# Sorting a token-choice expert layer in three stages instead of two

## The chip, the cores and the metric

The kernel runs on one core of one Trainium2 chip. The metric is device microseconds for one execution. One execution of each kernel is also taken by the hardware profiler, and its trace gives the rows below.

## The reference

One decoder layer over `x` of 2048 tokens by 256 features, with a context of 1601 rows:

```python
x = layernorm(x + linear_attention(x))            # 8 heads of 64
x = layernorm(x + cross_attention(x, ctx))        # 16 heads of 16
probs = softmax(x @ gate_w.T)                     # 16 experts
top_w, top_idx = top_k(probs, 4); top_w /= sum(top_w)
expert_e(x) = (silu(x @ w1[e].T) * (x @ w3[e].T)) @ w2[e].T    # hidden size 128
x = layernorm(x + sum_j top_w[j] * expert_top_idx[j](x) + shared_expert(x))
```

The change is in the last two lines, and in how they are woven into the cross attention ahead of them.

## The kernel before

The work has three parts in time: the linear attention (up to about 250 us), the cross attention (to about 802 us), and the experts (to the end).

**Cross attention.** Queries come in 4 chunks of 512 tokens, heads in 4 groups G of each chunk, keys in 13 tiles: 4 x 4 x 13 = 208 steps, 52 for each chunk (the text calls a step of the last chunk "step 9", and so on). In a step, `scores` makes four score tiles in a ring of banks, ScalarE takes their exponential (L937), and `weigh` (L1163) multiplies them with the values two steps later. Beside this TensorE makes two units of scores for a later group, and VectorE reduces them to a maximum (`read_max`, L1466). These units are 17 steps ahead, so that in the last chunk VectorE has them only up to step 34, and in the last group (from step 39) `weigh_whole` (L1177) takes wider tiles. When a group is through, `copy_num` on ScalarE (L852) empties the sum bank behind two of the four exponentials of the group's second step, and `weigh` of the next group waits for it. SyncE then moves the sums (`move_num`) and their denominators (`move_den`); VectorE inverts the denominators (`invert`, L1527).

**Gate and sort.** Behind each chunk stand the projection, the layer norm and the gate for its 512 tokens. Each token chooses 4 experts. A token's row is copied 4 times into DRAM (`sorted_d`), sorted by expert, in tiles of 128 rows that each belong to one expert. Tokens of the first three chunks are one batch (63 tiles, 12 token tiles), the last chunk another (31 tiles, 4 token tiles). For a batch `ranks` counts on TensorE how many choices of an expert stand ahead, `first_slots` and `slot_ends` work out on VectorE where each expert begins, `slot_of_choice` and `all_slots` give each choice its row, and `tile_owners` says which expert a tile has. The owners go to DRAM and back as one row of SBUF (`write_owner`, `load_owner`), since TensorE's sequencer reads them from one partition. GpSimd then issues one indirect DMA for each token tile and choice (`scatter`, L677); ahead of each round of choices it marks the rows (`mark`), which waits until the round before has landed. For the first batch these are 48 scatters, from step 32 of the last chunk on.

**Experts.** `WORK` is a fixed list of 110 tiles: 10 of the shared expert, the 63 of the first batch, 6 shared, the 31 of the second batch. Its index is i. All engines go through it in order. SyncE loads the sorted rows 6 tiles ahead (`load_tile`), and the first tile of a batch waits for all its scatters; from the thirteenth expert tile on, a load also waits until the result of an earlier tile has landed. GpSimd scatters each result back to its tokens (`give`, L685) at i + 3. The last chunk's projection, norm, gate and sort are placed at fixed i (6 to 35, and `SCATTER_AT` 37 to 67 on GpSimd). From i = 77 (`COMBINE_AT`) a token tile's four results are loaded (`load_given`), added, normalised and stored. The queue of SyncE is one list in program order, as are those of the other engines:

```python
if s == CHUNK_STEPS * (CHUNKS - 1) + 36: write_owner(0)
...
move_num(CHUNKS * GROUPS - 1)
move_den(CHUNKS * GROUPS - 1)
for i in range(-X_AHEAD, len(WORK) + BEHIND):
    if 0 <= i + X_AHEAD < len(WORK): load_tile(i + X_AHEAD)
```

On VectorE the last group's `invert` stands at i = 0, between the activations of tiles 1 and 2, and the last division at i = 4. On GpSimd `inverse_deviation` of chunk 2 (L665) stands ahead of the first scatter.

## Time and profile before

| | |
|---|---|
| median of 3 runs | 1096.03 us (1095.07 to 1097.78) |
| the profiled execution | 1086.56 us |
| its span | 1084.7 us |
| mean granted TensorE clock | 0.940 |
| TensorE busy | 951.4 us (88%) |
| VectorE busy | 732.9 us (68%) |
| ScalarE busy | 648.0 us (60%) |
| GpSimd busy | 254.6 us (23%) |

The span is the time from the first to the last instruction of the profiled execution; its own time stands 1.9 us above. The busy shares are means over three parts with different limits, so the views by stretch of time say more than this table.

### The profile page before, as it was taken

The page shows a single profiled execution, that of the slowest core. Times are in us where ns is not written, and L with a number is a line of the kernel's source. Part 1 is how long each engine was busy: PE and PEld are TensorE (multiplying, and loading weights), DVE is VectorE, ACT ScalarE, POOL GpSimd, SP SyncE. Part 2 cuts the span into 40 slices and gives each one's busy share as a digit, 9 for nine tenths or more (in the row PEclk, how much of TensorE's full clock was granted, in tenths as well). Part 3 has the DMA queues.
Part 4 walks back from the last instruction along what each step waited for, and adds up shares of the span by engine and source line. Part 5 has one row for each costly group of instructions (what it writes and reads, how often), then busy time and mean ns, then how long its engine had stood idle before and what let it go on. Part 6 is the DMA issues. An engine that isn't in the chain of part 4 may idle for free.

```text
span 1084.7 us, 19088 instructions
## 1 busy us (share of the span) xinstructions
PE 951.4 (88%) x6868; PEld 521.9 (48%) x6868; DVE 732.9 (68%) x1171; ACT 648.0 (60%) x1403; POOL 254.6 (23%) x306
## 2 busy tenths in 40 slices
PE   6997998779999999999999999998990698988890
PEld 2454566334444444444444444443340586776670
DVE  0206886798999998989989899889120343324773
ACT  1322223118888887878878788777870265654560
POOL 1006113600000000200002000000465255773654
PEclk9999999859999999999999999999895799999996
DMA  9007892200322112112211010011642246554763
GB/s 346 8 1 179 101 129 92 94 5 2 100 81 86 42 50 84 37 35 58 86 55 27 8 27 22 25 53 50 142 148 75 86 142 137 158 157 148 242 214 131
DMA packets 75800, 99.29 MB, mean 92 GB/s; under 512 B 17566, under 2 KB 58784, under 8 KB 75390
## 3 DMA queue, kind: packets, MB, share of 16 engines
q1 hardware_dynamic: 64252, 73.73, 26.8%
q0 software_dynamic: 7584, 20.79, 5.4%
q10 hardware_dynamic: 3872, 3.56, 1.0%
q8 instruction: 57, 0.93, 0.4%
q14 instruction: 35, 0.29, 0.1%
HBM read 52.45 MB, written 43.35 MB: 88 GB/s over the span
## 4 chain that ended last, share of the span: by engine, by line
PE 60%; DVE 17%; DMA 8%; issue 7%; POOL 6%; ACT 2%; SPq 0%; POOLq 0%; DVEq 0%; ACTq 0%
PE psum L1163 16%; PE psum L1053 13%; DVE mpart L1466 9%; PE psum L1149 7%; PE psum L1318 6%; POOL sorted_d L677 4%; PE psum L982 3%; PE psum L1336 3%; PE psum L1015 3%; DMA x_in<-sorted_d 2%; DMA given_d<-y_out,x_in 2%; PE psum L1279 2%; DMA sorted_d<-x_rows,slots 2%; PE psum L1103 1%; PE psum L1187 1%
## 5 line engine op out<-in xcount | busy, mean ns | idle before, releaser
L937 ACT ACTIVATE region<-psum 128x512 f32<-128x512 f32 (+1 forms) x832 | 448.6, 610 | 132.0 <-PE psum L1149 117.6
L1466 DVE TENSOR_REDUCE mpart<-psum 128x2 f32<-128x1024 f32 x384 | 461.7, 1222 | 39.4 <-PE psum L1053 36.4
L1163 PE MATMUL psum<-region 128*32 128x256 f32 (+1 forms) x3120 | 251.8, 395 | 7.4 <-ACT numT L852 7.4
L1053 PE MATMUL psum<-kstack,qstack 63*128 63x512 f32 (+1 forms) x1024 | 223.0, 463 | 19.9 <-DVE mpart L1466 19.5
L1053 PEld LDWEIGHTS psum<-kstack,qstack 63*128 63x128 f32 x1024 | 92.9, 194 | 194.0 <-issue 123.7
L1149 PE MATMUL psum<-qstack,kstack 64*128 64x512 f32 (+1 forms) x832 | 176.1, 412 | 0.1
L1683 DVE SCALAR_TENSOR_TENSOR silu_h<-tanh_h,psum 128x128 f32<-128x128 f32 x110 | 31.6, 287 | 150.7 <-ACT tanh_h L907 149.4
L1149 PEld LDWEIGHTS psum<-qstack,kstack 64*128 64x128 f32 (+1 forms) x832 | 111.3, 184 | 17.6 <-ACT region L937 14.5
L1163 PEld LDWEIGHTS psum<-region 128*32 128x32 f32 (+1 forms) x3120 | 62.2, 108 | 118.1 <-issue 75.7
L1318 PE MATMUL psum<-w_all,xT_in 128*128 x376 | 103.3, 399 | 3.8 <-issue 1.7
L685 POOL DMA_INDIRECT given_d<-y_out,x_in x94 | 93.4, 994 | 44.8 <-ACT y_out L921 27.3
L718 POOL TENSOR_TENSOR attnT<-num_c,den_c 128x512 f32<-128x512 f32 x7 | 8.9, 1278 | 357.7 <-DMA den_c<-den_d 357.6
L1279 PE MATMUL psum<-ident,x_in 128*128 128x128 f32 x188 | 38.0, 285 | 48.9 <-DMA x_in<-sorted_d 48.8
L901 ACT ACTIVATE xT_in<-psum 128x256 f32<-128x256 f32 x110 | 41.4, 378 | 59.9 <-PE psum L1279 59.7
L1318 PEld LDWEIGHTS psum<-w_all,xT_in 128*128 128x128 f32 x376 | 67.1, 198 | 12.4 <-issue 6.3
L677 POOL DMA_INDIRECT sorted_d<-x_rows,slots x64 | 62.3, 974 | 32.8 <-issue 29.6
L907 ACT ACTIVATE tanh_h<-psum 128x128 f32<-128x128 f32 x110 | 30.5, 277 | 54.2 <-PE psum L1318 53.8
L1336 PE MATMUL psum<-w_all,actT 128*128 x188 | 58.2, 393 | 0.3 <-ACT actT L913 0.3
L1279 PEld LDWEIGHTS psum<-ident,x_in 128*128 128x128 f32 x188 | 26.7, 148 | 61.8 <-issue 53.8
L921 ACT ACTIVATE y_out<-psum,x_in 128x256 f32<-128x256 f32 x94 | 44.5, 473 | 12.2 <-PE psum L1336 3.4
L665 POOL TENSOR_TENSOR rstd<-var_eps,half_neg 128x1 f32<-128x1 f32 (+1 forms) x20 | 14.4, 721 | 143.9 <-DVE var_eps L1559 73.5
L817 ACT ACTIVATE region<-region 128x512 f32<-128x512 f32 x16 | 10.1, 630 | 54.6 <-DVE region L1493 54.6
(172 smaller groups left out, 937.5 us busy)
## 6 DMA issues: line engine op xcount, KB each, us to landing
x_in<-sorted_d SPq DMA_DIRECT2D x94, 129.0 KB, 2.5
sorted_d<-x_in SPq DMA_DIRECT2D x7, 1548.0 KB, 7.3
given<-given_d SPq DMA_DIRECT2D x16, 512.0 KB, 4.6
qstack<-qparts_d SPq DMA_DIRECT2D x96, 64.0 KB, 2.3
kstack<-kparts_d SPq DMA_DIRECT2D x6, 800.5 KB
qparts_d<-region SPq DMA_DIRECT2D x4, 1024.0 KB, 4.1
kparts_d<-region SPq DMA_DIRECT2D x4, 800.5 KB, 10.1
xT<-in_xT SPq DMA_DIRECT2D x1, 2048.0 KB, 9.2
```

The costliest lines, as they stand in the source:

```text
L677: pool.indirect_dma_start(out=sorted_d[int(t >= GATE_FIRST)][:, :], out_offset=bass.IndirectOffsetOnAxis(ap=slots[:, t, j:j + 1], axis=0), ...
L685: pool.indirect_dma_start(out=given_d[int(v >= FIRST_SLOT[1])][:, :], out_offset=bass.IndirectOffsetOnAxis(ap=x_in[:, v % X_SLOTS, DIM:DIM ...
L901: act.activation(xT_in[:, i % 3, :], turn_bank("tile", i)[:, 0:DIM], ACT.Copy).then_inc(xT_copied, 1)
L921: act.activation(y_out[:, v % Y_SLOTS, :], bank(2 + i % 2)[:, 0:DIM], ACT.Copy, scale=x_in[:, v % X_SLOTS, DIM + 1:DIM + 2]).then_inc(y_co ...
L937: act.activation(prob[0:rows_of, s % 3, j, :], ring(n)[0:rows_of], ACT.Exp).then_inc(ring_read, 1)
L1053: mm = pe.matmul(bank(unit_bank(u) + side)[:, at * w:(at + 1) * w], qstack[rows_of, buffer(G), p, t * P:(t + 1) * P], kstack[rows_of, g * ...
L1149: pe.matmul(ring(n)[0:r], kstack[rows, g * PAIRS + p, kt * P:kt * P + r], qstack[rows, buffer(G), p, :], start=True, stop=True).then_inc(r ...
L1163: mm = pe.matmul(bank(NUM_BANK)[VW * j:VW * (j + 1), q], vals[0:r, g, kt, j, :], prob[0:r, s % 3, j, q], start=(kt == 0 and half == 0), st ...
L1279: mm = pe.transpose(turn_bank("tile", i)[:, k * P:(k + 1) * P], rows[:, k * P:(k + 1) * P], ident[:, :])
L1318: mm = pe.matmul(bank(6 + i % 2)[:, 0:2 * HID], xT_in[:, i % 3, k * P:(k + 1) * P], part_of(kind, v, k), start=(k == 0), stop=(k == DK - 1))
L1336: pe.matmul(bank(2 + i % 2)[:, 0:DIM], actT[:, i % 2, :], part_of(kind, v, DK), start=True, stop=True).then_inc(y_done, 1)
L1466: dve.tensor_reduce(mpart[:, G % 2, qt, :, p, n], both, X, ALU.max).then_inc(max_read, 1)
```

## The change

1. There are three sorting stages. Stage 0 holds the tokens of chunks 0 and 1 (8 token tiles), stage 1 those of chunk 2, stage 2 those of chunk 3. Stages 0 and 1 fill the same 63 tiles: an expert's choices of stage 1 first fill the room left in its tiles of stage 0, and the rest goes into more tiles behind (`open_more`). The order of these tiles is therefore not by expert alone, and `tile_owners` counts twice for this batch.
2. In the last chunk VectorE works out stage 0 at steps 7, 8 and 9, stage 1 at step 34, the owners at step 42; the ranks are made at steps 4 and 32. GpSimd issues 32 scatters for stage 0 in halves of 4 token tiles, then 16 for stage 1 in halves of 2, and each half has its own semaphore, so that `mark` waits for the same half of the round before. The deviation of chunk 2 is placed behind the third half.
3. The owners are worked out on all partitions along the free axis, straight into the row that TensorE's sequencer reads; the two DMAs through DRAM go.
4. `WORK` is reordered: 4 shared, 32 expert tiles, 6 times (1 shared, 3 expert), 13 expert, 6 times (1 shared, 2 expert), 19 expert. The loads of its first 14 entries (10 expert tiles) stand at step 50 of the last chunk in SyncE's queue, ahead of the last group's `move_num` and `move_den`. The scatters of stage 2 are at i = 37 to 59, 2 in 3 tiles, with 8 marks.
5. `copy_num` stands behind one exponential instead of two.
6. One semaphore for four experts' weights instead of one for each.

```diff
+STAGES = 3
+STAGE_OF = (0, 0, 1, 2)
+STAGE_BATCH = (0, 0, 1)
+STAGE_TILES = tuple(TPC * STAGE_OF.count(s) for s in range(STAGES))
+STAGE_FIRST = tuple(TPC * STAGE_OF.index(s) for s in range(STAGES))
+STAGE_HALF = tuple(n // 2 for n in STAGE_TILES)
...
-FIRST_SHARED = 10
-WORK = ([("shared", t) for t in range(FIRST_SHARED)] + [("expert", v) for v in range(SLOT_TILES[0])]
-        + [("shared", t) for t in range(FIRST_SHARED, TILES)]
-        + [("expert", v) for v in range(SLOT_TILES[0], ALL_SLOTS)])
+def mixed(pattern, shared, expert):
+    return [("shared", next(shared)) if kind == "s" else ("expert", next(expert)) for kind in pattern]
+_shared, _expert = iter(range(TILES)), iter(range(ALL_SLOTS))
+WORK = mixed("s" * 4 + "e" * 32 + "seee" * 6 + "e" * 13 + "see" * 6 + "e" * 19, _shared, _expert)
...
+LOADED_EARLY = 14
...
-                        + [(20, "x2T", 0), (21, "x2T", 1), (23, "logits", 0), (24, "logits", 1), (30, "rank", 0)])
+                        + [(4, "rank", 0), (20, "x2T", 0), (21, "x2T", 1), (23, "logits", 0), (24, "logits", 1),
+                           (32, "rank", 1)])
...
-        COMBINE_AT = {77 + (8 * t) // 3: t for t in range(GATE_FIRST)}
-        SCATTER_AT = {37 + 2 * k: divmod(k, TPC) for k in range(TOPK * TPC)}
+        COMBINE_AT = {78 + (8 * t) // 3: t for t in range(GATE_FIRST)}
+        SCATTER_AT = {37 + (3 * k) // 2: divmod(k, TPC) for k in range(TOPK * TPC)}
...
-            def write_owner(b):
-                sp.wait_ge(owner_ready, b + 1)
-                sp.dma_start(owner_d[b:b + 1, :].rearrange("o p -> p o"), owner[:, b:b + 1]).then_inc(owner_written, 16)
-            def load_owner(b):
-                sp.wait_ge(owner_written, 16 * (b + 1))
-                sp.dma_start(owner_row[0:1, b, :], owner_d[b:b + 1, :]).then_inc(owner_loaded, 16)
...
-                        sp.wait_ge(scattered, 16 * TOPK * (FIRST_TOKEN[b] + TOKEN_TILES[b]))
+                        for stage in range(STAGES):
+                            if STAGE_BATCH[stage] == b:
+                                for half in range(2):
+                                    sp.wait_ge(scattered[stage][half], 16 * TOPK * STAGE_HALF[stage])
...
-                if s == CHUNK_STEPS * (CHUNKS - 1) + 36:
-                    write_owner(0)
-                if s == CHUNK_STEPS * (CHUNKS - 1) + 45:
-                    load_owner(0)
+                if s == STEPS - 2:
+                    for i in range(LOADED_EARLY):
+                        load_tile(i)
...
-                if 0 <= i + X_AHEAD < len(WORK):
+                if LOADED_EARLY <= i + X_AHEAD < len(WORK):
                     load_tile(i + X_AHEAD)
-                if i == 36:
-                    write_owner(1)
-                if i == 42:
-                    load_owner(1)
...
+            def mark(stage, half, j):
+                n = STAGE_HALF[stage]
+                at = STAGE_FIRST[stage] + half * n
+                first = at - FIRST_TOKEN[STAGE_BATCH[stage]]
+                if j >= 1:
+                    pool.wait_ge(scattered[stage][half], 16 * j * n)
                 link(pool.iota(x_rows[:, at:at + n, DIM:DIM + 1].bitcast(I32).rearrange("p t o -> p (t o)"),
-                               pattern=[[P * TOPK, n]], base=j, channel_multiplier=TOPK))
+                               pattern=[[P * TOPK, n]], base=first * P * TOPK + j, channel_multiplier=TOPK))
...
+            def sort_half(stage, half, j):
+                mark(stage, half, j)
+                for t in range(STAGE_HALF[stage]):
+                    scatter(stage, half, STAGE_FIRST[stage] + half * STAGE_HALF[stage] + t, j)
+            def sortable(stage):
+                pool.wait_ge(x2_ready, STAGE_FIRST[stage] + STAGE_TILES[stage])
+                pool.wait_ge(slots_ready, stage + 1)
...
-            pool.wait_ge(x2_ready, GATE_FIRST)
-            pool.wait_ge(slots_ready, 1)
+            sortable(0)
             for j in range(TOPK):
-                if j >= 1:
-                    pool.wait_ge(scattered, 16 * j * GATE_FIRST)
-                mark(0, j)
-                for t in range(GATE_FIRST):
-                    scatter(t, j)
-                if j == 1:
-                    divide(CHUNKS - 1, 0)
+                for half in range(2):
+                    sort_half(0, half, j)
+                    if j == 1 and half == 0:
+                        inverse_deviation(c_var, c_rstd, CHUNKS - 2, TPC)
+            sortable(1)
+            for j in range(TOPK):
+                for half in range(2):
+                    sort_half(1, half, j)
+            divide(CHUNKS - 1, 0)
...
+                    half, first = divmod(t, STAGE_HALF[2])
+                    if j == 0 and t == 0:
+                        sortable(2)
+                    if first == 0:
+                        mark(2, half, j)
+                    scatter(2, half, GATE_FIRST + t, j)
...
-                    if j == 2:
+                    if j == 1:
...
-                pe.wait_ge(owner_loaded, 16 * (b + 1))
+                pe.wait_ge(owner_ready, b + 1)
...
-                    if v < EXPERTS:
-                        pe.wait_ge(ld_we[v], 16 * 3)
+                    if v < EXPERTS and v % 4 == 0:
+                        pe.wait_ge(ld_we[v // 4], 16 * 3 * 4)
...
+            def open_tiles(stage):
+                rank_known(stage)
+                n = STAGE_TILES[stage]
+                link(dve.tensor_scalar(tiles_of[:, :], rank[:, n, :], (P - 1) / 2, 1.0 / P, ALU.add, ALU.mult))
+                link(dve.tensor_scalar(tiles_of[:, :], tiles_of[:, :], ROUND, ROUND, ALU.add, ALU.subtract))
+                link(dve.tensor_scalar(tiles_of[:, :], tiles_of[:, :], 1.0, None, ALU.max))
+                link(dve.tensor_tensor_scan(ends[:, :], tiles_of[:, :], zero_gate[:, 0, :], 0.0, ALU.add, ALU.add))
+                link(dve.tensor_tensor(start[:, :], ends[:, :], tiles_of[:, :], ALU.subtract))
+                link(dve.tensor_scalar(start[:, :], start[:, :], float(P), None, ALU.mult))
+                if stage == 0:
+                    link(dve.tensor_copy(count[:, :], rank[:, n, :]))
+                    link(dve.tensor_scalar(room[:, :], tiles_of[:, :], float(P), None, ALU.mult))
...
+            def open_more(stage):
+                rank_known(stage)
+                n = STAGE_TILES[stage]
+                link(dve.tensor_tensor(tiles_of[:, :], rank[:, n, :], count[:, :], ALU.add))
+                link(dve.tensor_tensor(tiles_of[:, :], tiles_of[:, :], room[:, :], ALU.subtract))
+                link(dve.tensor_scalar(tiles_of[:, :], tiles_of[:, :], 0.0, (P - 1) / 2, ALU.max, ALU.add))
+                link(dve.tensor_scalar(tiles_of[:, :], tiles_of[:, :], 1.0 / P, None, ALU.mult))
+                link(dve.tensor_scalar(tiles_of[:, :], tiles_of[:, :], ROUND, ROUND, ALU.add, ALU.subtract))
+                link(dve.tensor_tensor_scan(more_ends[:, :], tiles_of[:, :], zero_gate[:, 0, :], 0.0, ALU.add, ALU.add))
+                link(dve.tensor_scalar(more_ends[:, :], more_ends[:, :], ends[:, EXPERTS - 1:EXPERTS], None, ALU.add))
+                link(dve.tensor_tensor(jump[:, :], more_ends[:, :], tiles_of[:, :], ALU.subtract))
+                link(dve.tensor_scalar(jump[:, :], jump[:, :], float(P), None, ALU.mult))
+                link(dve.tensor_tensor(jump[:, :], jump[:, :], room[:, :], ALU.subtract))
+                link(dve.tensor_tensor(jump[:, :], jump[:, :], start[:, :], ALU.subtract))
...
+            def slot_of_choice(stage):
+                n = STAGE_TILES[stage]
+                r, hot, past = rank[:, 0:n, :], one_hot[:, 0:n, :, :], over[:, 0:n, :]
+                if stage == 1:
+                    link(dve.tensor_tensor(r, r, by_token(count[:, :], n), ALU.add))
+                    link(dve.tensor_tensor(past, r, by_token(room[:, :], n), ALU.is_ge))
+                    link(dve.tensor_tensor(past, past, by_token(jump[:, :], n), ALU.mult))
+                    link(dve.tensor_tensor(r, r, past, ALU.add))
+                link(dve.tensor_tensor(r, r, by_token(start[:, :], n), ALU.add))
...
+            def passed(b, to, after):
+                n = SLOT_TILES[b]
+                link(dve.tensor_tensor(
+                    over[:, 0:n, :], by_token(after, n),
+                    tile_no[:, 0:n].rearrange("p (t o) -> p t o", o=1).broadcast_to([P, n, EXPERTS]), ALU.is_le))
+                link(dve.tensor_reduce(to, over[:, 0:n, :], X, ALU.add))
+            def tile_owners(b):
+                n = SLOT_TILES[b]
+                first, other = who[:, 0, 0:n], who[:, 1, 0:n]
+                passed(b, first, ends[:, :])
+                if b == 0:
+                    link(dve.tensor_scalar(other, first, EXPERTS - 0.5, -float(EXPERTS), ALU.is_ge, ALU.mult))
+                    link(dve.tensor_tensor(first, first, other, ALU.add))
+                    passed(b, other, more_ends[:, :])
+                    link(dve.tensor_tensor(first, first, other, ALU.add))
+                link(dve.tensor_scalar(first, first, float(EXPERTS - 1), float(W_PARTS), ALU.min, ALU.mult))
+                link(dve.tensor_scalar(other, first, W_PARTS * BELOW - 0.5, float(W_PARTS * W_GAP), ALU.is_ge, ALU.mult))
+                dve.tensor_tensor(owner_row[:, b, 0:n], first, other, ALU.add).then_inc(owner_ready, 1)
             def activate(i):
                 h = bank(6 + i % 2)
...
-                    if at == 31:
-                        first_slots(0)
-                        slot_ends(0)
-                    if at == 32:
+                    if at == 7:
+                        open_tiles(0)
+                    if at == 8:
                         slot_of_choice(0)
+                    if at == 9:
                         all_slots(0)
-                    if at == 33:
+                    if at == 34:
+                        open_more(1)
+                        slot_of_choice(1)
+                        all_slots(1)
+                    if at == 42:
                         tile_owners(0)
             for i in range(-AHEAD, len(WORK) + BEHIND):
                 if i == 27:
                     gate_chosen(CHUNKS - 1)
                 if i == 31:
-                    first_slots(1)
...
                 if i == 31:
-                    first_slots(1)
+                    open_tiles(2)
                 if i == 32:
-                    slot_ends(1)
+                    slot_of_choice(2)
                 if i == 33:
+                    all_slots(2)
+                if i == 35:
                     tile_owners(1)
-                if i == 34:
-                    slot_of_choice(1)
-                if i == 35:
-                    all_slots(1)
                 if i - 2 in COMBINE_AT:
                     give_out(COMBINE_AT[i - 2])
                 if i in COMBINE_AT:
```

## Rows read from the trace of the kernel before

**Rows 1.** The page's clock in 40 slices, and the waits from 780 us on.

```profile
PEclk9999999859999999999999999999895799999996
PE psum L1279 <- DMA x_in<-sorted_d: 48.8, 7, 34.1
```

**Rows 2.** Timeline of TensorE: start, duration, instructions, idle before and its releaser.

```profile
850.00 0.66 PE L1279 MATMUL psum<-ident,x_in 128*128 128x128 f32 x2 [34.14 <-DMA x_in<-sorted_d]
...
915.96 0.41 PE L1279 MATMUL psum<-ident,x_in 128*128 128x128 f32 x2 [4.37 <-DMA x_in<-sorted_d]
```

**Rows 3.** Timeline of GpSimd, out of the first batch's 48 scatters.

```profile
759.87 1.23 POOL L677 DMA_INDIRECT sorted_d<-x_rows,slots  x1 [0.45 <-POOL x_rows L674]
...
770.87 0.97 POOL L677 DMA_INDIRECT sorted_d<-x_rows,slots  x1 [2.17 <-issue]
...
785.36 0.15 POOL L672 IOTA x_rows<- 128x12 int32 x1 [8.47 <-DMA sorted_d<-x_rows,slots]
...
845.37 0.97 POOL L677 DMA_INDIRECT sorted_d<-x_rows,slots  x1 [0.31 <-issue]
```

**Rows 4.** Timeline of SyncE's queue.

```profile
802.88 0.60 SPq L482 DMA_DIRECT2D den<-numT  x1
...
847.81 6.58 SPq L546 DMA_DIRECT2D x_in<-sorted_d  x12
```

**Rows 5.** The view by tile of numT: durations in ns, and who waited for it.

```profile
L852 ACT ACTIVATE numT<-psum x16: 597/605/605, 278.3 to 802.3; 128x512 f32<-128x512 f32 x16
...
  PE psum L1163: 7.4, 13
```

**Rows 6.** Timeline of VectorE around the first batch's sort, and the last inversion.

```profile
752.29 0.35 DVE L1639 TENSOR_TENSOR over<-rank,steps_of 128x192 f32<-128x192 f32 x1
...
758.66 0.19 DVE L1676 CAST slots<-which 128x48 int32<-128x48 f32 x1
...
761.88 0.16 DVE L1659 TENSOR_TENSOR owner<-small 128x1 int32<-128x1 f32 x1
...
764.73 0.21 DVE L1523 STREAM_TRANSPOSE negT<-negmax 128x32 f32<-128x32 f32 x1
...
806.44 0.24 DVE L1527 RECIPROCAL den<-den 128x16 f32<-128x16 f32 x1
```

**Rows 7.** Timeline of VectorE in steps 9 to 12, at step 17 and at step 19.

```profile
681.50 9.88 DVE L1466 TENSOR_REDUCE mpart<-psum 128x2 f32<-128x1024 f32 x8
...
710.43 0.17 DVE L1559 TENSOR_SCALAR var_eps<-meanvar 128x4 f32<-128x4 f32 x1
...
715.19 1.30 DVE L1555 TENSOR_SCALAR x_rows<-x_rows,meanvar,rstd 128x256 f32<-128x256 f32 x4
```

**Rows 8.** The view by tile of rank, its multiply by one_hot (ns).

```profile
L1669 DVE TENSOR_TENSOR one_hot<-one_hot,rank x2: 425/692/959, 756.7 to 905.7; 128x768 f32<-128x768 f32 x1, 128x256 f32<-128x256 f32 x1
```

**Rows 9.** The view by tile of owner_d, and busy time by window.

```profile
DMA to landing us min/median/max: 8.3/8.6/9.0
912.00:914.00 2.00, 0.00 (x0) 0.00 (x0) 0.00 (x1) 0.10 (x1) 1.69 (x2) 1.00 0.86 45
```

**Rows 10.** The chain that ended last: a result on its way to DRAM.

```profile
986.64 3.39 DMA given_d<-y_out,x_in
```

**Rows 11.** Windows (PE, PEld, DVE, ACT, POOL busy, clock, DMA share, GB/s).

```profile
757.00:763.00 6.00, 3.70 (x32) 1.88 (x30) 5.46 (x11) 2.28 (x5) 2.87 (x5) 0.75 0.37 107
850.00:875.00 25.00, 24.77 (x122) 20.45 (x123) 11.98 (x40) 12.16 (x41) 5.95 (x6) 0.89 0.30 85
```

**Rows 12.** Timeline of ScalarE: the tanh of tiles 43, 55, 78 and 79, of 110.

```profile
923.93 0.28 ACT L907 ACTIVATE tanh_h<-psum 128x128 f32<-128x128 f32 x1 [0.34 <-PE psum L1318]
...
943.46 0.28 ACT L907 ACTIVATE tanh_h<-psum 128x128 f32<-128x128 f32 x1 [0.34 <-PE psum L1318]
...
990.24 0.28 ACT L907 ACTIVATE tanh_h<-psum 128x128 f32<-128x128 f32 x1 [0.48 <-PE psum L1318]
997.60 0.28 ACT L907 ACTIVATE tanh_h<-psum 128x128 f32<-128x128 f32 x1 [2.76 <-PE psum L1318]
```

More of the change, by code:

```diff
@@ L240, in decoder_layer @@
         y_out = sb("y_out", [P, Y_SLOTS, DIM])
-        one_hot = sb("one_hot", [P, GATE_FIRST, TOPK, EXPERTS])
-        rank = sb("rank", [P, GATE_FIRST + 1, EXPERTS])
-        over = sb("over", [P, EXPERTS, GATE_FIRST])
-        ends = sb("ends", [P, 2, EXPERTS])
+        one_hot = sb("one_hot", [P, STAGE_TILES[0], TOPK, EXPERTS])
+        rank = sb("rank", [P, STAGE_TILES[0] + 1, EXPERTS])
+        over = sb("over", [P, SLOT_TILES[0], EXPERTS])
+        who = sb("who", [P, 2, SLOT_TILES[0]])
+        tiles_of, ends, start, room, count, more_ends, jump = (
+            sb(name, [P, EXPERTS]) for name in ("tiles_of", "ends", "start", "room", "count", "more_ends", "jump"))
         def sems(*names):
```

133 lines of the change are left out of this document (48 added, 85 removed).

## The prediction

> **What bounds the kernel now.** I read the clock in slices first. In slices 30 and 31 (about 813 to 868 us) it falls to 0.5 and 0.7 [rows 1]: TensorE has nothing to do there. The waits name it: TensorE waited 48.8 us in 7 places for sorted rows, once for 34.1 us [rows 1]. The timeline puts that wait at 816 to 850 us [rows 2], behind the shared tiles that can run without sorted rows. The queue of GpSimd shows why: the scatters start at 759.9 us and the last is issued at 845.4 us, 48 of them [rows 3], and SyncE's loads start 1.5 us behind it [rows 4]. So the sort of three chunks is too late by 34 us, and what ends it is GpSimd's issue, one scatter each 1.27 us.
>
> Elsewhere the bound is different. In the cross attention VectorE runs without a pause (8 reductions in 9.88 us, [rows 7]), so whatever is put on it before step 34 lengthens the step. In the experts the pace is 1.63 us a tile (12 tiles between the first two tanh of [rows 12]); 110 tiles would be 179 us. In fact tile 79 comes 7.36 us behind tile 78 (these jumps, here and below, are differences between successive starts of the 110 tanh, of which [rows 12] shows four). Such jumps stand where a result's scatter lands late and holds SyncE's queue.
>
> **The change part by part.** All against the profiled execution (1086.6 us, which is 0.9% below the median of the runs).
>
> *Sums copied earlier.* TensorE waits 7.4 us in 13 places for the copy of the sums, 0.57 us each; the copy takes 0.60 us [rows 5]. Moving it ahead of one exponential (in the same timeline 0.55 us) ends it that much sooner, at the moment TensorE wants it. It needs the last weighing of the group before, which TensorE ends at about the time the first exponential ends; so I take 0.5 us of the 0.57 in each place: **-6.5** (0 to -7.4). It ends at 0 if ScalarE then sits waiting for that weighing and the second exponential comes late by as much.
>
> *Work for the slots, on VectorE while it bounds.* Removed before step 34: from 752.29 to the next reduction 1.6 us, 2.4 us up to behind the cast at 758.66, and 0.9 us up to behind the owners at 761.88 [rows 6], 5.0 us together, all between reductions without idle time. Added at steps 7 to 9: eight small instructions at a pitch of 0.21 (that of the small ones in [rows 6]'s stretch), one add (0.3), and a multiply and a reduction over 512 elements, which lie between the 0.43 us for 256 and 0.96 us for 768 [rows 8], so 0.7 each, and a cast: 3.6 us. Stage 1's part (11 small instructions, 5 adds, multiply and reduction over 256, cast: 4.7 us) and the owners (two or four passes over up to 1008 elements, about 7 us) come behind step 34, where VectorE has no reductions left; that idle stretch hides them. Net **-1.4** (-5.0 if TensorE hides the new ones, 0 if the new ones cost more).
>
> *The dip.* From 757 to 763 us the clock was at 0.75 [rows 11], with TensorE busy 3.7 of 6 us while VectorE was at the slots. 3 of these 6 us at half speed lose 1.5 us, and it takes about as long again until the clock is back. The pieces now put there are smaller: **-2** (0 to -3). The ranks on TensorE (14 small matmuls in two places instead of 13 in one) I leave at 0.
>
> So the attention ends 10 us sooner.
>
> *The gap.* Stage 0 needs its slots at step 9 (about 686 us on the old clock). Its 32 scatters go at 1.27 us; each seventh is followed by a pause of 2.17 instead of 0.30 us [rows 3], which makes 1.55 each. With marks it takes under 60 us with room to spare: stage 1's slots are ready at 764.9 - 10 + 4.7 = 759.6 us. Then 16 scatters at 1.55 (25 us) and 8 marks at 0.75 (6 us): 790.6. Waits for landing: between 0 and three times 8.5 us, the one case in which weights were being loaded [rows 3]. Each half's round is only 3.3 us, so part of this will be seen, but the owners' DMA that stood in this stretch is gone: I take 4. Landing 1.5: all is sorted at **796 us**. The attention now ends near 792. The whole 34.1 us gap goes, and the restart behind it: a mean clock of 0.89 over 25 us [rows 11] is 5.5 us at half speed, 2.7 us lost. Together **-36.8**.
>
> *What is late next.* SyncE now has the wait for these scatters and ten loads at step 50, and `move_num` and `move_den` of the last group are queued behind. Ten loads at 0.55 us (12 took 6.58, [rows 4]) end at 801.6; the sums' denominators, issued then, land within 2.5 us: 804.2. VectorE's last inversion stands at i = 0, ran at 806.44 [rows 6], and would be wanted at 796.4. VectorE waits 7.8 us there, the activation of tile 2 is queued behind it, and TensorE and ScalarE wait for that. With a little clock lost: **+9** (+4 with no landing waits, +30 with all three).
>
> *Deviation of chunk 2 on GpSimd.* It stands behind 12 scatters (19 us, so at about 706 us), while the variances come at 710.4 and their user at 715.2 [rows 7]. It is in time by some 8 us; it costs nothing, but holds the other 20 scatters until about 712, which stage 0 can bear.
>
> *Owners without DRAM.* The write took 8.3 to 9.0 us to land, and with it in flight the 16 engines were 86% busy at 45 GB/s [rows 9]. A load of sorted rows issued beside it kept TensorE waiting 4.37 us at 915.96 [rows 2]; tile 40 came 6.5 us behind tile 39, and 41 3.1 us behind that, 6.3 us over the pace: **-6.3** (-4.4 to -6.3). The DMA page of the Trainium skill, "DMA: Bandwidth & Descriptors", section on the anatomy of one DMA, gives a fixed 2.0 us plus bytes over bandwidth; by that, 0.5 KB would land in 2 us, hinder nothing, and this term would be near 0 and the time some 6 us longer. The row says otherwise, so the row is used.
>
> *GpSimd's backlog.* At i = 37 to 67 it had 31 results, 16 scatters and 4 marks: 47 x 1.275 + 4 x 1.1 = 64 us in 31 x 1.63 = 50.5 us of tiles; the 14 us surfaced as two jumps (4.0 and 4.9 us over the pace around tiles 56 and 68). Now, at i = 37 to 59, 17 results, 16 scatters, 8 marks: 51 us in 37.5 us. The same 13.5 us, but a load waits for the result 12 expert tiles back, which is now 16 places back, so that some 5 us more is forgiven: **-4** (0 to -9).
>
> *End of batch 0.* Tile 79's jump (7.36 and the next 2.35 against 1.63 each: 6.4 us over) came because the result at 986.64 landed 3.39 us later [rows 10, 12] while SyncE waited for all results; GpSimd was 3 us behind. It now has 20 places to catch up, and the wait stands one tile later: **-6** (0 to -6.4). A last such jump, 5.0 us around tile 95, is met with the gaps of the shared tiles before it: **-2.5** (0 to -5).
>
> *The rest* (last tile to end, four loads, combine, store), some 25 us, and one semaphore for four experts: 0.
>
> Sum: -6.5 - 1.4 - 2 - 36.8 + 9 - 6.3 - 4 - 6 - 2.5 = **-56.5**, so 1030 us for a profiled execution. Times 1096.03 / 1086.56: **1039 us**.
>
> **The rivals.**
> *A, the sort is late.* Stage 1's rounds of 2 token tiles are too short to cover the landing. For it: the 8.47 us wait; against: other landings took 1.5 us. With the full +30 it gives 1060 us.
> *B, nothing late at the start.* Scatters land in 1.5 us and the backlog is forgiven wholly: +4 instead of +9, -9 instead of -4, -5 instead of -2.5, so 1026; with a little more from the attention 1022.
> *C, slower, by a port.* If VectorE's instructions held back GpSimd's descriptors, the sort would be paid at VectorE's pace, now that it runs beside 94%-busy reductions. Everything hangs on the one wait in SyncE's queue. The change ends slower than before when all is sorted later than 796 + 57 = 853 us, that is, when stage 1's scatters take (853 - 759.6 - 7.5) / 16 = 5.4 us each. The first scatter, which began during a reduction, took 1.23 us against 0.97 [rows 3], so the rows bear out 0.3 us and not 4: the time would be 1039 + 5 at that. At 5.4 us it would be 1096 or more. The Trainium skill, "SBUF — State Buffer", section on two separate sides, describes such a lock: a VectorE instruction in a two-port mode shuts GpSimd out, descriptor writes too. The trace agrees at most in the size of 0.3 us.
> *D, no change.* The experts' part is bound by GpSimd's queue whatever comes before, and the 34 us return as backlog. For it: 94 results and 16 scatters at 1.275 us are 140 us; against: the tiles take 179 us. It would give 1090 us.
>
> **How the numbers follow.** Forecast 0.56, A 0.19, B 0.17, C 0.03, D 0.03, and 0.02 for a loss of another kind. The likeliest case gives 1039. The forecast alone spans 1027 to 1050; with A and B, and leaving a tenth on each side, 1022 to 1061. A measurement tells 0.3% from nothing, about 3 us. Faster: forecast, A, B and most of D, 0.95; same 0.02; slower 0.03.
>
> **What would show it.** The 34 us idle stretch gone and a first expert tile right behind the fourth shared tile; the waits for numT under 1 us; VectorE's inversion preceded by an idle of some 8 us for `den`; the last scatter of stage 1 near 795 us; no jump near tile 40; smaller jumps near tiles 56 to 80. The prediction is wrong if the wait at i = 0 is over 25 us, if the attention does not end by 795 us, or if jumps of GpSimd's making come back in the mixed part.

## The result, and the profile after

The changed kernel took 1079.8 us (median of 4 runs, 1075.8 to 1081.1) beside 1095.6 us (4 runs, 1094.8 to 1097.8) for the kernel before: a ratio of 0.984, 95% interval 0.981 to 0.987. It is faster, by 16 us where I had forecast 57, and outside my range (1022 to 1061). The profiled execution took 1079.2 us, its span is 1077.3.

First the rows that came as forecast. From the page of the changed kernel (clock by slice; then the matmuls of the weighing, whose idle time was 7.4 us before, [rows 5]) and from its timelines of SyncE and ScalarE:

```profile
PEclk9999999858999999999999999985999999999995
...
L1177 PE MATMUL psum<-region 128*32 128x256 f32 (+1 forms) x3120 | 254.3, 399 | 1.8
```

```profile
821.17 4.73 SPq L553 DMA_DIRECT2D x_in<-sorted_d  x10
830.53 0.61 SPq L494 DMA_DIRECT2D den<-numT  x1
```

```profile
829.91 0.60 ACT L863 ACTIVATE numT<-psum 128x512 f32<-128x512 f32 x1 [1.19 <-PE psum L1191]
...
832.18 0.28 ACT L921 ACTIVATE tanh_h<-psum 128x128 f32<-128x128 f32 x1 [0.48 <-PE psum L1332]
```

The wait for the sums is gone, and so is the 34 us wait for sorted rows [rows 2]: the loads stand at 821 us, before the attention ends. But the first number of the last fence is late. The last copy of the sums, which ends the attention, comes at 829.9 us. It was at 802.3 [rows 5] and I wanted it near 792. From that copy to the end of the span it is 247.4 us instead of 282.4. So the gap was closed, and the attention lost 28 us against the kernel before and 38 against the forecast.

Where in the attention? Four marks of the last chunk: the negated maxima of steps 8, 22 and 34 (VectorE's transposes into `negT`) and the last copy. From VectorE's timeline of the changed kernel, with the variances of chunk 2 between the first two:

```profile
677.31 0.21 DVE L1537 STREAM_TRANSPOSE negT<-negmax 128x32 f32<-128x32 f32 x1
...
716.89 0.17 DVE L1573 TENSOR_SCALAR var_eps<-meanvar 128x4 f32<-128x4 f32 x1
...
742.41 0.21 DVE L1537 STREAM_TRANSPOSE negT<-negmax 128x32 f32<-128x32 f32 x1
...
787.70 0.21 DVE L1537 STREAM_TRANSPOSE negT<-negmax 128x32 f32<-128x32 f32 x1
```

In the table the first column is the time of that mark, the others are distances between marks, in us.

| | step 8 | 8 to 22 | 22 to 34 | 34 to last copy |
|---|---|---|---|---|
| before | 681.2 | 39.6 | 43.9 | 37.5 |
| changed | 677.3 | 65.1 | 45.3 | 42.2 |

Up to step 8 the change gains 3.9 us. Then it loses 25.5 us in the stretch in which GpSimd issues nearly all of stage 0's 32 scatters. GpSimd's timeline in it:

```profile
683.48 1.22 POOL L681 DMA_INDIRECT sorted_d<-x_rows,slots  x1 [0.46 <-POOL x_rows L678]
...
698.57 0.97 POOL L681 DMA_INDIRECT sorted_d<-x_rows,slots  x1 [0.30 <-issue]
717.15 1.04 POOL L665 TENSOR_TENSOR rstd<-var_eps,half_neg 128x4 f32<-128x4 f32 x1 [17.61 <-DVE var_eps L1573]
...
718.85 1.06 POOL L681 DMA_INDIRECT sorted_d<-x_rows,slots  x1 [0.29 <-POOL x_rows L678]
...
744.89 0.96 POOL L681 DMA_INDIRECT sorted_d<-x_rows,slots  x1 [0.30 <-issue]
```

Two rows, of 12 and of 20 scatters. Against [rows 3] the pause behind each seventh is missing. And this is what the timelines of VectorE, ScalarE and TensorE show inside the second row:

```profile
724.91 1.23 DVE L1480 TENSOR_REDUCE mpart<-psum 128x2 f32<-128x1024 f32 x1 [0.83 <-PE psum L1067]
733.55 0.71 DVE L1476 TENSOR_REDUCE mpart<-psum 128x8 f32<-128x528 f32 x1 [7.41 <-remote]
741.41 0.71 DVE L1476 TENSOR_REDUCE mpart<-psum 128x8 f32<-128x528 f32 x1 [7.15 <-remote]
```

```profile
733.64 1.09 ACT L951 ACTIVATE region<-psum 128x512 f32<-128x512 f32 x2 [5.24 <-remote]
...
734.29 0.79 PE L1163 MATMUL psum<-qstack,kstack 64*128 64x512 f32 x1 [4.94 <-ACT region L951]
```

VectorE and ScalarE stand still for 5 to 7 us at a time. The releaser is given as "remote", which names no instruction of the program. TensorE stands with them: from 729.4 to 733.5 us none of the three does anything, and it starts last, behind ScalarE. Windows of the two rows, changed kernel (the columns are those of [rows 11]), and one inside the second:

```profile
690.00:706.00 16.00, 13.22 (x58) 5.30 (x58) 6.25 (x8) 6.37 (x13) 7.35 (x10) 0.68 0.22 73
718.00:748.00 30.00, 16.95 (x107) 7.41 (x107) 9.16 (x15) 7.82 (x14) 21.51 (x31) 0.64 0.27 95
...
730.00:733.00 3.00, 0.00 (x0) 0.00 (x0) 0.00 (x0) 0.00 (x0) 2.39 (x3) 0.50 0.25 88
```

In the second, VectorE was busy 9.2 of 30 us; in [rows 7] its reductions ran without a pause. The DMA engines are only 27% busy, so their bandwidth isn't used up. The granted clock, 0.68 and 0.64 in the two windows, is part of the loss and comes behind the idle time: from 690 to 693 us it was still 1.00 with TensorE busy 2.2 of 3 us and VectorE 1.2, and from 696 us it was 0.50. These are the 8 and the 5 in the page's clock line. How much of the loss is the clock's, no run separates.

### The profile page after: what moved, and what is told of

The parts are those of the page before. It is cut to its first block, busy times and chain, and to the rows that moved or that the text cites. A ratio compares the mean times of both kernels' runs of the same rounds, so it can differ in the third digit from the quotient of the medians.

```text
span 1077.3 us, 19150 instructions
## 1 busy us (share of the span) xinstructions
PE 959.6 (89%) x6869; PEld 522.0 (48%) x6869; DVE 742.8 (69%) x1197; ACT 648.3 (60%) x1404; POOL 260.5 (24%) x337
## 4 chain that ended last, share of the span: by engine, by line
PE 69%; DVE 18%; issue 6%; DMA 4%; ACT 2%; another core or an unknown queue 1%; POOL 1%; SPq 0%; POOLq 0%; DVEq 0%; ACTq 0%
PE psum L1177 17%; PE psum L1067 13%; DVE mpart L1480 10%; PE psum L1163 9%; PE psum L1332 8%; PE psum L1350 4%; PE psum L996 3%; PE psum L1029 3%; PE psum L1293 2%; PE psum L1201 1%; PE psum L1117 1%; DMA kparts_d<-region 1%; PE psum L1340 1%; DMA x_in<-sorted_d 1%; PE psum L1003 1%
## 5 line engine op out<-in xcount | busy, mean ns | idle before, releaser
L1480 DVE TENSOR_REDUCE mpart<-psum 128x2 f32<-128x1024 f32 x384 | 460.8, 1222 | 50.5 <-PE psum L1067 40.4
L1163 PE MATMUL psum<-qstack,kstack 64*128 64x512 f32 (+1 forms) x832 | 185.3, 417 | 16.5 <-issue 11.2
L1163 PEld LDWEIGHTS psum<-qstack,kstack 64*128 64x128 f32 (+1 forms) x832 | 114.7, 185 | 40.2 <-issue 23.7
L1332 PE MATMUL psum<-w_all,xT_in 128*128 x376 | 100.0, 389 | 9.2 <-issue 7.6
L996 PE MATMUL psum<-xT,region 128*128 128x512 f32 x64 | 30.7, 645 | 10.2 <-DMA region<-in_L_attn_Wk 10.2
```

The lines of the kernel that those rows point to most:

```text
L996: mm = pe.matmul(bank(4 * (f % 2) + n), wk_s[:, k, f * P:(f + 1) * P], xT[:, k, n * CHUNK:(n + 1) * CHUNK], start=(k == 0), stop=(k == DK ...
L1163: pe.matmul(ring(n)[0:r], kstack[rows, g * PAIRS + p, kt * P:kt * P + r], qstack[rows, buffer(G), p, :], start=True, stop=True).then_inc(r ...
L1332: mm = pe.matmul(bank(6 + i % 2)[:, 0:2 * HID], xT_in[:, i % 3, k * P:(k + 1) * P], part_of(kind, v, k), start=(k == 0), stop=(k == DK - 1))
L1480: dve.tensor_reduce(mpart[:, G % 2, qt, :, p, n], both, X, ALU.max).then_inc(max_read, 1)
```

## The experiments

My theory S: unbroken scatters hold up the other engines. The rival R: something else in the change does (the earlier copy, the slots' work).

**1. Scatters held back until VectorE has no more reductions.**

```diff
+            inverse_deviation(c_var, c_rstd, CHUNKS - 2, TPC)
             sortable(0)
+            pool.wait_ge(slots_ready, 2)
             for j in range(TOPK):
                 for half in range(2):
                     sort_half(0, half, j)
-                    if j == 1 and half == 0:
-                        inverse_deviation(c_var, c_rstd, CHUNKS - 2, TPC)
```

The deviation of chunk 2 moves ahead of the scatters with it.

> The changed kernel with its first scatters held back until the slots of stage 1 are known, so that all 48 follow VectorE's last reduction of the attention, as in the kernel before; nothing else is undone. Theory S (the two bursts of stage 0's scatters, 12 and 20 in a row beside scores, exponentials and reductions, slow every other engine): the copy of the last sums comes near 793 to 797 us instead of 829.9, the 48 scatters run from about 762 to about 830, the experts wait for them some 30 us, and the time is 1072 to 1085 us. Rival R (the earlier copy of the sums, or VectorE's longer slot work, is what slows the attention): the copy of the last sums stays later than 820 us, and the time is over 1095 us.

Measured: 1084.7 us, ratio 0.990 (0.986 to 0.994). The time is the one that I gave for S, and the mark is the one that I gave for R: the last copy came at 830.9 us. Steps 8 to 22 took 41.4 and 22 to 34 38.8 us, so what had been slow was cured with the early copy still in place; but step 34 to the last copy, now beside the scatters, took 75.6 us. Windows of that kernel:

```profile
765.00:790.00 25.00, 16.75 (x104) 5.10 (x106) 2.06 (x6) 13.75 (x28) 18.72 (x28) 0.78 0.64 204
```

and of the kernel before:

```profile
765.00:790.00 25.00, 24.73 (x191) 8.95 (x187) 0.25 (x1) 23.68 (x48) 9.99 (x12) 0.96 0.66 155
```

The loss went where the scatters went. It hardly needs VectorE either: VectorE had 2.06 us of work there, and TensorE and ScalarE lost all the same. What I had not reckoned with: the kernel before has its scatters in this very stretch, and its profile shows no loss (37.5 us from step 34 on).

**2 to 4. The kernel before with 32 transfers more**: as scatters in the places of stage 0's, as direct transfers from GpSimd's queue in the same places, and as direct transfers from SyncE's, two at each of the steps 10 to 25. The direct ones write the same rows of DRAM as the scatters, 32 apart. The call of each:

```diff
+                pool.indirect_dma_start(out=extra_d[:, :],
+                                        out_offset=bass.IndirectOffsetOnAxis(ap=extra_at[:, k:k + 1], axis=0),
+                                        in_=x_sb[:, k % 8, :], in_offset=None).then_inc(extra_done, 16)
...
+                pool.dma_start(extra_d.rearrange("(p n) w -> p n w", n=EXTRAS)[:, k, :],
+                               x_sb[:, k % 8, :]).then_inc(extra_done, 16)
...
+                if 10 <= now < 26:
+                    sp.wait_ge(pv_done, s - 1)
+                    for k in (2 * (now - 10), 2 * (now - 10) + 1):
+                        sp.dma_start(extra_d.rearrange("(p n) w -> p n w", n=EXTRAS)[:, k, :],
+                                     x_sb[:, k % 8, :]).then_inc(extra_done, 16)
```

> The kernel before with 32 more scatters of 128 rows (1,024 bytes each, into a DRAM tensor of their own, rows spread over 4,096) from GpSimd's queue in the last chunk: 12 from step 9, 20 behind the inverse deviation of step 17; nothing else is changed. Theory S: the copy of the last sums comes 25 to 30 us later than 802 us, and the time is 1095.5 + 25 to 30 = 1120 to 1126 us. Rival R: the copy of the last sums stays within 3 us of 802, and the time is 1095 to 1099 us.

> As the run with 32 more scatters, but each is a direct transfer of the same 128 rows from GpSimd's queue, with no list of indices. If it is GpSimd's making of descriptors, or the queue that it feeds, that disturbs the others: 1115 to 1126 us, as with the scatters. If it is the indices (their reading, or writes to spread rows): 1095 to 1099 us. Rival R: 1095 to 1099 us too.

> As the run with 32 more direct transfers, but from SyncE's queue, two at each of the steps 10 to 25 of the last chunk: the same bytes in the same stretch and none of GpSimd's work. If it is the traffic (bytes to DRAM or the DMA engines' time): 1115 to 1126 us. If it is GpSimd's own work or queue: 1095 to 1100 us, the copy of the last sums within 4 us of 802.

Measured, on one chip with the first experiment: 1116.3 us (ratio 1.018, 1.014 to 1.023) with scatters, 1092.2 (0.998, 0.996 to 1.000) with direct transfers of GpSimd's, 1092.9 (0.999, 0.996 to 1.001) with SyncE's; the kernel before took 1094.2. The scatters cost 22 us, less than the 25 to 30 that I had written, with the last copy at 829.0 us, as written. So S holds, and it is the indirect form: the same 128 rows of 1,024 bytes, to the same places, cost nothing in the time as direct transfers, from either queue. (In both of these runs the last copy came later than I had allowed, at 808.5 and 807.6 us; what that was shows only below.) Two windows of each, first with scatters, then direct from GpSimd:

```profile
682.00:706.00 24.00, 20.92 (x148) 8.69 (x145) 14.57 (x16) 13.60 (x27) 12.06 (x13) 0.86 0.20 68
718.00:748.00 30.00, 24.68 (x172) 11.83 (x172) 15.81 (x20) 14.12 (x27) 18.34 (x20) 0.79 0.34 112
```

```profile
682.00:706.00 24.00, 23.55 (x206) 10.75 (x204) 20.79 (x24) 18.76 (x37) 6.71 (x12) 1.00 0.34 106
718.00:748.00 30.00, 27.83 (x265) 13.85 (x269) 26.06 (x46) 22.37 (x44) 5.87 (x11) 1.00 0.42 124
```

More bytes per second (106 and 124 GB/s against 68 and 112), and VectorE at 20.8 and 26.1 us as in the kernel before (20.9 and 26.05 there). But GpSimd is also done with a direct one much sooner (12 in 6.71 us, against 12.06 with one other instruction), so "less of GpSimd's work" is not told apart from "no list of indices".

**5 to 8. A pace, neighbouring rows, and the copy.** The pace in the changed kernel (`pv_done` counts the steps whose weighing TensorE has finished):

```diff
                 for t in range(STAGE_HALF[stage]):
+                    k = (2 * j + half) * STAGE_HALF[stage] + t
+                    pool.wait_ge(pv_done, LAST_CHUNK + (9 + (7 * k) // 10 if stage == 0 else 36 + k))
```

> The changed kernel with its scatters spread over the steps of the last chunk: scatter k of stage 0 waits for step 9 + 0.7 k of that chunk (one about each 2.3 us), scatter k of stage 1 for step 36 + k; nothing else is changed. Theory P (unbroken rows of more than about five scatters disturb, single ones don't): the copy of the last sums comes near 792 to 798 us instead of 829.9, the last scatter lands about 802, and the time is 1042 to 1056 us. Theory N (each scatter beside the attention costs the others about 1 us, whatever lies between them): 40 or more scatters beside the attention cost about what they did, the copy stays later than 820 us, and the time is 1072 to 1085 us.

> The kernel before with the same 32 more scatters as in the run that gave 1116.3 us, but each waits for its own step (9 + 0.7 k of the last chunk). Theory P: within 4 us of the kernel before (1094 to 1099 us). Theory N: 1112 to 1120 us.

> As the run with 32 more scatters in rows of 12 and 20, but each one's indices are 128 neighbouring rows instead of rows 32 apart. If the spread of the rows in DRAM is what costs: 1094 to 1100 us. If it is the form of the instruction (the list of indices): 1111 to 1119 us, as with spread rows.

> The changed kernel with the copy of the sums again behind the second exponential (j == 2), as in the kernel before. My prediction gave the earlier copy 6.5 us: then 1079.8 + 6.5 = 1086 us, with 7 us again before the matmul that follows the copies. Rival: the attention loses its time elsewhere and the copy is worth nothing: 1078 to 1082 us. A harmful early copy: under 1077 us.

Measured: 1035.8, 1081.9, 1084.5 and 1034.6 us, and the kernel before beside them 1084.3. All were without loss, the fifth faster than either case that I had written and the eighth far inside that of a harmful early copy, and two of them should not have been: the seventh has the same unbroken rows of 12 and 20, and the eighth, the changed kernel with only the copy put back, came out 45 us under the changed kernel. Its last copy of the sums stands at 795.3 us with GpSimd's rows as unbroken as ever. Either the copy and the spread of the rows matter in a way that I could not think of, or this chip was another. The kernel before took 10 us less than on the first. So none of the four says anything on the pace, on the rows or on the copy's share of the loss.

**9 to 12. The same kernels again, beside the changed one.**

> The changed kernel as it is, beside the next three on one chip. So far the kernels with unbroken scatters that lost 22 to 28 us beside the attention (the changed kernel, 1079.8 us; the one held back, 1084.7; 32 spread scatters more, 1116.3) ran on one chip or two, and the kernels without a loss, two of them with the same unbroken scatters (1034.6 and 1084.5 us), on another, on which the kernel before takes 1084.3 us instead of 1094 to 1096. Theory C (the chip decides whether an unbroken row of scatters disturbs the other engines): where the kernel before takes about 1084 us, this one takes 1030 to 1037 us, and where it takes about 1095, 1075 to 1085. Theory K (the kernel decides: the earlier copy and spread rows are what it takes): 1075 to 1085 us wherever it runs.

> The kernel before with 32 more scatters to spread rows, which gave 1116.3 us beside 1094.2, again. Theory C: where the kernel before takes about 1084 us, within 3 us of it; where it takes about 1095, 1110 to 1120. Theory K: 18 to 24 us over the kernel before, wherever it runs.

> The changed kernel with the later copy of the sums, which gave 1034.6 us, again. Theory C: where the kernel before takes about 1084 us, 0 to 7 us over the changed kernel; where it takes about 1095, 1075 to 1092. Theory K: 1030 to 1045 us wherever it runs, far under the changed kernel.

> The changed kernel with spread scatters, which gave 1035.8 us, again. Theory C with the pace as the cure: within 3 us of the changed kernel where that has no loss, and 1042 to 1058 us where it has one. Theory C without a cure: 1072 to 1085 us there.

Measured: 1031.4, 1085.5, 1037.3 and 1037.4 us; the kernel before took 1086.8. That is theory C (only the last missed: 6.0 us over the changed kernel, where I had written 3). **The changed kernel, word for word the same, took 1031.4 us here: a ratio of 0.949, 0.945 to 0.953.** The kernel with 32 scatters more took 1116.3 us on one chip and 1085.5 on another (ratios 1.018 and 1.000). The last copy of the sums of that kernel in the view by tile, first trace and second:

```profile
L869 ACT ACTIVATE numT<-psum x16: 597/603/604, 278.0 to 829.0; 128x512 f32<-128x512 f32 x16
```

```profile
L869 ACT ACTIVATE numT<-psum x16: 597/603/603, 278.9 to 799.6; 128x512 f32<-128x512 f32 x16
```

And the changed kernel's windows on this chip, to be held against the two shown first:

```profile
690.00:706.00 16.00, 14.91 (x130) 6.88 (x122) 13.49 (x19) 12.22 (x24) 7.00 (x9) 1.00 0.41 126
718.00:748.00 30.00, 27.44 (x263) 12.70 (x265) 26.53 (x46) 22.91 (x46) 14.70 (x20) 1.00 0.46 139
```

The granted clock is 1.00 in both windows. I call a chip of the first kind disturbed and one of the second kind quiet; that the difference lies in the chip is taken up at the end.

**13 to 15. Looking for a disturbed chip**, to learn whether a pace cures.

> The changed kernel as it is, beside the next two on one chip: 1030 to 1037 us where unbroken scatters disturb nothing (the kernel before about 1084 there), 1075 to 1085 us where they do (about 1095).

> The changed kernel with one scatter to a step or so. If the pace is a cure (rows of five and more are what disturbs): 1042 to 1058 us where the changed kernel takes 1075 to 1085, and 2 to 7 us over it where it takes 1030 to 1037. If each scatter disturbs by itself there: within 8 us of the changed kernel.

> The kernel before with 32 more scatters to neighbouring rows. On a chip where scatters disturb: 16 to 24 us over the kernel before if the spread of the rows plays no part, within 4 us of it if it is what costs. On one where they don't: within 4 us.

Measured: 1036.3, 1036.6 and 1086.0 us, the kernel before 1086.8: a quiet chip, and no answer. (The changed kernel's ratio was 0.954 here, 0.949 to 0.959, from two runs.)

**16. A row and a pace in one trace.** The first 12 scatters unbroken, the rest paced, so that the trace tells by itself what kind of chip it is from.

```diff
...
+                    if stage == 1 or k >= 12:
+                        pool.wait_ge(pv_done, LAST_CHUNK + (18 + (7 * (k - 12)) // 10 if stage == 0 else 36 + k))
```

> The changed kernel with its first 12 scatters in an unbroken row, as they are, and the other 20 of stage 0 spread over the steps 18 to 31 (one about each 2.3 us), those of stage 1 one to a step: one trace that shows by its first row whether the chip is one on which scatters disturb, and by the rest whether spread ones do. Nothing lost in the first row: such a chip again, 1031 to 1039 us, no answer. Lost in the first row (the negated maxima of step 34 late, ScalarE and VectorE idle from 689 us): with the pace as cure 1044 to 1058 us, the loss ending with the row at about 705 us; if each scatter disturbs: 1068 to 1082 us.

Measured: 1054.0 us (two runs), the kernel before 1096.3 (ratio 0.961, 0.958 to 0.965), and the trace is from a disturbed chip. The time lies where I had written it for a cure. The row of 12, then the paced scatters:

```profile
690.00:706.00 16.00, 11.07 (x60) 4.60 (x58) 5.96 (x8) 5.71 (x11) 7.36 (x10) 0.80 0.23 76
718.00:748.00 30.00, 29.12 (x278) 14.27 (x280) 25.82 (x37) 23.66 (x46) 15.30 (x23) 1.00 0.30 94
```

VectorE's variances (which GpSimd's deviation waits for) and maxima in it:

```profile
677.36 0.21 DVE L1542 STREAM_TRANSPOSE negT<-negmax 128x32 f32<-128x32 f32 x1
...
716.60 0.17 DVE L1578 TENSOR_SCALAR var_eps<-meanvar 128x4 f32<-128x4 f32 x1
...
726.99 0.21 DVE L1542 STREAM_TRANSPOSE negT<-negmax 128x32 f32<-128x32 f32 x1
...
766.21 0.21 DVE L1542 STREAM_TRANSPOSE negT<-negmax 128x32 f32<-128x32 f32 x1
```

| changed kernel | 8 to 22 | 22 to 34 | 34 to last copy |
|---|---|---|---|
| quiet | 41.8 | 38.8 | 36.9 |
| disturbed | 65.1 | 45.3 | 42.2 |
| disturbed, row of 12, then paced | 49.6 | 39.2 | 37.3 |

The row of 12 costs 7.8 us, and 36 scatters at a mean pace of 2.1 us, three of them back to back at most, cost 0.8 us together. So the pace is the cure for the attention, by one trace in which both kinds of scatter stand. It is not one for the rest: from its last copy to the end of the span this kernel took 249.7 us, against 236.8 in the quiet trace of the changed kernel, and most of that lies between tiles 36 and 60 (52.2 against 40.0 us), beside stage 2's unpaced scatters.

**17, 18. The paced kernel again, and the paced kernel with stage 2's scatters wider apart** (`36 + 2 * k` instead of `37 + (3 * k) // 2`).

> The changed kernel with spread scatters beside the attention, now that a trace from a disturbed chip shows a row of 12 to cost about 9 us and the spread ones nothing. Where the kernel before takes about 1095 us: the copy of the last sums at 793 to 796 us and 1042 to 1047 us in all (10 us of loss left in the expert tiles, where stage 2's scatters and the gives run back to back). Where it takes about 1085: 1034 to 1038.

> As the one beside it, and the scatters of stage 2 stand at every second tile from tile 36 instead of at 1.5 tiles from 37, so that GpSimd has 1.5 instead of 1.67 indirect transfers to a tile (1.27 us each, by a pace of 1.63 us a tile). If unbroken rows disturb: on a disturbed chip 3 to 8 us under the one beside it; on another chip within 3 us of it.

Measured: 1037.1 and 1035.0 us (ratios 0.956, 0.953 to 0.958, and 0.953, 0.950 to 0.956), the kernel before 1085.4: a quiet chip again. Both are as good as the changed kernel is on such a chip, within 6 us; on a disturbed one neither was run.

## Why the prediction was wrong

**Where scatters disturb nothing, the sum came true, in part by errors that cancelled.** The trace before has a last copy at 802.3 us and no loss beside its scatters, so it is one of the quiet kind, and the sum was made against it: -56.5 us. On one quiet chip the medians are 1086.8 and 1031.4 us, -55.4; on another 1086.8 and 1036.3, -50.5. Step by step, from the changed kernel's trace of the first of them:

```profile
792.55 4.61 SPq L553 DMA_DIRECT2D x_in<-sorted_d  x10
797.26 0.61 SPq L494 DMA_DIRECT2D den<-numT  x1
```

```profile
794.10 0.60 ACT L863 ACTIVATE numT<-psum 128x512 f32<-128x512 f32 x1 [1.19 <-PE psum L1191]
796.36 0.28 ACT L921 ACTIVATE tanh_h<-psum 128x128 f32<-128x128 f32 x1 [0.48 <-PE psum L1332]
...
799.65 0.25 DVE L1541 RECIPROCAL den<-den 128x16 f32<-128x16 f32 x1 [1.28 <-DMA den<-numT]
```

- *Sums copied earlier*, -6.5. With the copy put back, TensorE again waits for it, and the time is 1037.3 against 1031.4: 6.0 us, with ranges that just overlap (1034.0 to 1040.0 and 1030.0 to 1034.5). Not all of it may be the copy's: the last copy came only 3.7 us later there (797.8), and on two other quiet chips the kernel with the late copy (1034.6) and the changed one (1036.3) have the same ratio, 0.954. From the view by tile of numT with the copy put back:

```profile
  PE psum L1177: 7.4, 13
```

- *Attention 10 us sooner*: 8.2 (794.1). The whole gap went, as forecast.
- *What is late next*, +9: 2. The last scatter was issued by 791 us and SyncE's loads began at 792.6, where I had 796 (one landing was waited for 1.33 us, another 0.31, where I took 4), so SyncE was through its ten loads at 797.2 and VectorE sat idle 1.3 us for the denominators, not 7.8. Tile 4 came 0.8 us over the pace and tile 7 1.3 us later than before.
- *Owners*, -6.3: tiles 40 and 41 stand at the pace. Right.
- *Backlog*, -4: -2.2. The jumps moved to tiles 58, 64, 66 and 67, 6.7 us over the pace together, against 8.9.
- *End of batch 0*, -6: -1.8, from which 1.1 at tile 82 go off again. A jump of 5.76 us is there still, at tile 74. *The last jump*, -2.5: -2.3.

From the first tanh to the last it was 251.7 us before and 206.1 now, -45.6, where the forecast's terms behind the attention make -46.6. That they agree so well is luck: the start cost 7 us less than I had put down, and the end of batch 0 and the backlog gave 5 and 2 us less.

**The step that failed is in "The gap": "Its 32 scatters go at 1.27 us".** The rate came true. But I asked only whether the scatters would be in time, and nowhere what they do to the engines that they now run beside: that term stood at nothing, without a reason. On a disturbed chip the missing term is +38 us in the attention (829.9 against 792) and +11 in the experts (247.4 against 236 to the end of the span); 1030 + 49 is 1079. In the experts it seems to be the same thing. From i = 37 to 59 stage 2's scatters and the results stand mostly at 1.27 us back to back. From tile 36 to tile 60 the changed kernel took 56.0 us here, and with its scatters held back or partly paced on a disturbed chip 52.2 both times, against 40.0 in its two quiet traces; 5 us come back behind. The list of waits of the changed kernel has, from 815 to 1000 us (total, times, longest; "issue" is time in which the profile shows nothing that the engine waited for),

```profile
DVE silu_h L1730 <- issue: 38.0, 28, 4.3
...
PEld psum L1350 <- issue: 12.6, 11, 3.1
```

with tile 51 5.76 us behind tile 50. The quiet trace lists no such wait of VectorE's. That these too are the scatters' doing is argued from place and kind; the run that would have told it (18) fell on a quiet chip.

**The last step failed with it**: "Times 1096.03 / 1086.56". I took the 0.9% as a difference between profiled and other runs. It was most likely the same disturbance. The two disturbed chips of the experiments gave the kernel before 1094.2 and 1096.3 us, the four quiet ones 1084.3 to 1086.8; and in the two traces of the disturbed chip in which the kernel before has only direct transfers more, the stretch from step 34 to the last copy, beside its own scatters, took 44.8 and 45.4 us, against 37.5. That stretch isn't what lengthens the time, though, since the wait for sorted rows takes it up again: tile 9, just behind that wait, comes at 855.6 and 853.1 us in the same two traces, against 856.5. What stays is in the experts, beside the last chunk's scatters: 55.2 and 57.1 us from tile 36 to tile 60, against 46.4 to 49.7 in three quiet traces. By the times, the kernel before pays about 9 us on a disturbed chip, and the changed one about 45.

**Rival C** had the right suspicion (an exchange between GpSimd's descriptors and VectorE) and the wrong direction: I asked whether VectorE holds back the scatters. It doesn't; inside a row a scatter is issued each 1.27 us in both traces, in the quiet one with VectorE busy 26.5 of 30 us. On a disturbed chip the scatters hold back the others.

## What to carry to other kernels

Moving work into the shadow of another engine's needs a term for what that work does to the engines it now runs beside, above all for a long unbroken run of indirect DMAs: with one wait on a counter of the main loop to each, they cost 0 to 6 us more where unbroken ones lost nothing, and where those lost 35 us beside the attention, pacing 36 of the 48 brought the loss to 9 (one trace). When a change gives 5% on one chip and 1.5% on another, compare traces of one program from both before explaining either. And an offset between the profiled execution and the runs is a measurement to explain, not a factor to multiply by.

## What the hardware showed that I had not expected

- Chips differ in this: of six on which experiments ran, two showed the loss in every trace and four in none. What differs in them no trace here tells. No chip was used twice, and each was used for one sitting, so whether it is the chip, its hour or something else that was fixed for a sitting is not shown.
- On a disturbed chip the loss sets in some 6 us after the first scatter of a row (689 us for one that began at 683.5, about 725 for 718.9) and ends within some 5 us of the last (one trace). The changed kernel's first row, 12 scatters in 16 us, cost the attention 8 us (its variances 39.6 us behind step 8's maxima, against 31.4 on a quiet chip), the second, 20 in 27 us, about 22.
- The Trainium skill, "SBUF — State Buffer", section on two separate sides, names the port that GpSimd and VectorE share as the one place where engines contend, and says of the others that they don't wait. The held-back kernel's loss can't be explained by that port: with VectorE busy only 2.06 of 25 us, ScalarE was busy 13.75 and TensorE 16.75, against 23.7 and 24.7 in the kernel before. Whether the two stood at a port of SBUF at all, no trace shows.
- Open: whether it is the list of indices or GpSimd's longer work on each scatter, whether scatters to neighbouring rows disturb less (run twice, both on quiet chips; direct transfers to spread rows cost nothing on a disturbed one), how much of the 45 us a fully paced kernel keeps on a disturbed chip, and what unit it is.
